# First attention of a four-layer graph kernel: the scaled rows, the logits and the routing choice of older groups are put ahead of the mixing in the orders of ACT, PE and DVE

## The reference

```
h = rmsnorm(layernorm(x), ln1_w)
q, k, v = h @ wq.T, h @ wk.T, h @ wv.T      # 4 heads of 32, 2 kv heads
q, k = rotated(q), rotated(k)
att = softmax(causal(q @ k.T / sqrt(32)))
x2 = layernorm(x) + (att @ v) @ wo.T
flat = rmsnorm(x2, ln2_w)
probs = softmax(flat @ router_w.T)          # 8 experts
tp, ti = top_k(probs, 2)                    # the routing choice
```

## Time and profile before

| | |
|---|---|
| median of 3 runs | 1738.74 us (1738.03 to 1741.6) |
| profiled execution | 1740.67 us |
| its span | 1738.7 us |
| busy in the span | PE 1287.0, DVE 1017.5, POOL 812.2, ACT 740.3 us |
| mean granted TensorE clock | 0.882 of full speed |
| the first attention | from about 380 to 747 us of the span |

### The profile page before, as it was taken

How to read it: one execution, slowest core, us unless ns; L and a number is a source line. 1 busy time by engine, 2 the same in 40 slices (tenths; PEclk the granted TensorE clock), 3 DMA queues, 4 the chain that set the end, 5 groups by cost and what they waited for, 6 DMA issues and landing times. The chain is left out here.

```text
span 1738.7 us, 34925 instructions
## 1 busy us (share of the span) xinstructions
PE 1287.0 (74%) x8909; PEld 1090.6 (63%) x8909; DVE 1017.5 (59%) x3818; ACT 740.3 (43%) x1710; POOL 812.2 (47%) x839
## 2 busy tenths in 40 slices
PE   3988888837677777349999995767773299999930
PEld 2777666726566667238888884545552189888920
DVE  1788888757767776335555553888885122222236
ACT  2555555515655555214444441443432155555510
POOL 3255555561455554614444443277676144445420
PEclk9999999968989988669999997888876599999975
DMA  6100000000000000145656563122211366766647
GB/s 157 23 1 0 0 0 0 1 1 1 20 28 28 25 25 27 40 133 190 201 189 199 191 201 105 55 71 73 71 36 41 104 214 219 218 217 220 218 133 203
DMA packets 134763, 168.57 MB, mean 97 GB/s; under 512 B 17584, under 2 KB 105520, under 8 KB 134704
## 3 DMA queue, kind: packets, MB, share of 16 engines
q1 hardware_dynamic: 98224, 122.49, 23.6%
q0 software_dynamic: 17408, 35.95, 5.9%
q10 hardware_dynamic: 19072, 9.46, 1.9%
HBM read 123.47 MB, written 44.37 MB: 97 GB/s over the span
## 5 line engine op out<-in xcount | busy, mean ns | idle before, releaser
L1602 POOL DMA_INDIRECT rows<-m_yb,m_dsti x288 | 276.6, 960 | 361.1 <-DVE m_dsti L1734 312.5
L1627 PE MATMUL psum<-m_xT,m_w 128*128 128x256 f32 (+1 forms) x864 | 200.2, 381 | 1.3 <-ACT m_xT L1668 1.3
L964 POOL DMA_INDIRECT dispatch<-a_flat,a1r_pos x128 | 129.9, 1015 | 111.4 <-DVE a1r_pos L945 69.4
L964 POOL DMA_INDIRECT dispatch<-g_flat,g1r_pos x128 | 133.2, 1041 | 74.3 <-DVE g1r_pos L945 37.3
L1627 PEld LDWEIGHTS psum<-m_xT,m_w 128*128 128x128 f32 (+1 forms) x864 | 149.1, 179 | 28.9 <-ACT m_xT L1668 1.9
L1701 DVE TENSOR_TENSOR m_yb<-psum,m_w 128x256 f32<-128x256 f32 x72 | 30.6, 425 | 218.6 <-PE psum L1642 218.6
L1683 ACT ACTIVATE m_sg<-psum,m_w 128x256 f32<-128x256 f32 x288 | 117.9, 471 | 92.4 <-PE psum L1632 91.3
L1632 PE MATMUL psum<-m_xT,m_w 128*128 128x256 f32 x576 | 141.2, 389 | 7.4 <-ACT m_xT L1666 7.4
L1642 PE MATMUL psum<-m_w,m_sg 128*128 128x128 f32 x1152 | 140.5, 275 | 0.6 <-DVE m_yb L1701 0.6
L1676 ACT ACTIVATE m_sg<-psum 128x256 f32<-128x256 f32 (+1 forms) x216 | 78.8, 382 | 142.9 <-PE psum L1627 98.5
L1717 DVE TENSOR_TENSOR m_hT<-psum,m_sg 128x256 f32<-128x256 f32 (+1 forms) x216 | 88.4, 422 | 83.7 <-ACT m_sg L1676 81.1
(11 more groups left out here) (250 smaller groups left out, 2971.2 us busy)
## 6 DMA issues: line engine op xcount, KB each, us to landing
m_w<-in_c_wall SPq DMA_DIRECT2D x72, 578.0 KB, 3.6
m_w<-in_c_wall SPq DMA_DIRECT2D x72, 533.0 KB, 3.4
m_xg<-dispatch SPq DMA_DIRECT2D x144, 130.0 KB, 3.5
g1c_y<-rows SPq DMA_DIRECT2D x32, 256.0 KB
fin_y<-rows ACTq DMA_DIRECT2D x32, 256.0 KB, 3.5
rows<-m_yb,m_dsti POOLq DMA_INDIRECT x288, 3.1
out<-x SPq DMA_DIRECT2D x16, 256.0 KB, 3.0
dispatch<-nobody SPq DMA_DIRECT2D x24, 130.0 KB, 6.8
```

The source lines that it names most:

```text
L964: pool.indirect_dma_start(out=dest, out_offset=bass.IndirectOffsetOnAxis(ap=self.pos[:, k, p:p + 1], axis=0), in_=flat[:, p, :], in_offset ...
L1602: pool.indirect_dma_start(out=rows_out, out_offset=bass.IndirectOffsetOnAxis(ap=dsti[j][:, t:t + 1], axis=0), in_=yb[j][:, t, :], in_offse ...
L1627: i = pe.matmul(bank[0:cn, TILE * m:TILE * m + TILE], w[j][:, HID * m + c0:HID * m + c0 + cn], xT[j % 2][:, :], start=(m == 0), stop=True, ...
```

## The change

Three of the four `step` functions of the first attention get another order. No instruction is added, removed or altered.

```diff
--- before.py
+++ after.py
@@ -1197,17 +1197,17 @@
                 def step(g, b):
                     scores(g)
                     head_T(g + 1)
+                    out_T(g - 1)
                     if runs(g - 3):
                         R.tensor_rank(pe, g - 3, bR)
-                    out_T(g - 1)
                     project(g + 1)
                     out_product(g - 1)
+                    flat_T(g - 2, b)
                     probs_T(g, 0)
                     probs_T(g, 1)
-                    flat_T(g - 2, b)
+                    logits(g - 2)
                     turned_T(g + 1)
                     mix(g, b)
-                    logits(g - 2)
                 skewed(pe, step, first=4)
 
             @block.scalar
@@ -1307,14 +1307,14 @@
 
                 def step(g, b):
                     head_T(g + 1)
+                    out_flat(g - 2, b)
+                    out_T(g - 1)
                     exp(g, 0)
                     exp(g, 1)
-                    out_T(g - 1)
-                    head_v(g + 1, 1 - b)
-                    out_flat(g - 2, b)
+                    flat_T(g - 2)
                     probs_T(g, 0)
                     probs_T(g, 1)
-                    flat_T(g - 2)
+                    head_v(g + 1, 1 - b)
                     turned_T(g + 1)
                     head_h(g + 2)
                     out_squares(g - 1)
@@ -1429,11 +1429,11 @@
                     rotated(g + 1, 0)
                     rotated(g + 1, 1)
                     out_x2(g - 1)
+                    if runs(g - 2):
+                        R.vector_choose(dve, g - 2, bR, True)
                     head_stats(g + 3)
                     norm(g)
                     out_ms(g - 1)
-                    if runs(g - 2):
-                        R.vector_choose(dve, g - 2, bR, True)
                 skewed(dve, step, first=4, ahead=3)
                 R.vector_weights(dve, True)
```

## The result

| | before | changed |
|---|---|---|
| median of 4 runs | 1740.17 us (1738.03 to 1743.23) | 1692.07 us (1689.4 to 1699.41) |
| profiled execution, its span | 1740.67, 1738.7 | 1699.41, 1697.5 |
| mean granted clock | 0.882 | 0.879 |

The ratio is 0.9726, 95% interval 0.9696 to 0.9756: 48 us saved, against the 49 of the forecast (1690). The profiled execution of the changed kernel is the slowest of its four; its mean granted clock is 0.879, that of the three others 0.889 to 0.895. Its span is 41.2 us shorter than the one before. It divides so: the first a_mx of the attention is at 403.22 before and 403.43 now, the experts' first DVE instruction at 747.37 and 705.70, and what follows takes 991.3 and 991.8. The whole difference of the two profiled executions lies in the attention, 344.2 us before, 302.3 now.

The account below looks back on a forecast made before the run. A 20.0 us chain across DVE, ACT and PE was taken to pace each turn; without 5.1 us of it DVE would. Savings of 41.7 + 1 + 5.1 + 0.7, say 49 us, gave 1690 us, range 1683 to 1712.

Parts of the forecast that it names:

- The chain and what leaves it: First attention's turn: a 20.0 us chain through DVE, ACT and PE; choice, a_flat and its transpose, together 5.1 us, leave it.
- DVE's 16.33 us as the new bound: Steady turns: DVE's own work paces them, taken as 16.5 us instead of 20.3, saving 41.7 us over 11 turns.
- the rank costs its own few tenths and DVE reads it only after its soft part. Nothing.: PE's rank matmuls, moved behind out_T: no longer held until the choice's end, they add no time to the turn.
- The mixing's margin: PE's mixing done at about +13.6 us of a step, DVE wants it at +14.0: 0.4 us to spare, called pessimistic.
- The logits' margin: PE's logits ready at +8.0 us, DVE wants them at +8.6: 0.6 us to spare, the forecast's thinnest margin.
- POOL: Root and scatters covered by 0.9 us per turn; in the tail, blocks 12.4 us apart, saving 5.1 and 0.7 us.
- The choice beside the scatters: DVE's choice, now beside POOL's scatters, costs nothing; the rival that it holds them up had 5 in 100, 9 us less saved.
- Sum: Whole kernel: 41.7 + 1 + 5.1 + 0.7 = 48.5, say 49 us saved, giving 1690 us by the median.
- The slower rival: PE's clock falls, PE becomes the bound, 3 us above the old turn, about 1770 us; 4 in 100.
- The signs: Trace marks of a right forecast: turn near 16.5 us, DVE busy over 95 in 100, PE's clock 0.95 or more.

Follow-up runs that it names:

- e1: Kernel before with only DVE's order changed (choice moved ahead of the next statistics and norm): 1779.89 us, ratio 1.0202 to the kernel before.
- e2: Changed kernel with DVE's old order put back, so only ACT's and PE's orders new: 1724.83 us, ratio 0.9889 to the kernel before.
- e3: Changed kernel with ACT's old order put back, DVE's and PE's new: 1787.37 us, ratio 1.0260 to the kernel before.
- e8: Changed kernel with PE's rank matmuls directly behind the scores, ahead of head_T and out_T: 1698.59 us, ratio 0.9759 to the kernel before.
- e4: Changed kernel with ACT's copy of v back ahead of fT and the probabilities: 1715.98 us, ratio 0.9849 to the kernel before.

## Why the prediction was right, by its own steps

- **The chain and what leaves it.** Right. The reciprocal's 3.8 us are gone, and e1 to e3 show that the orders belong together: DVE's alone and the other two without ACT's are slower than before, and ACT's and PE's without DVE's bring less than half. PE's order wasn't left out by itself.
- **DVE's 16.33 us as the new bound.** Right for every second turn: 16.46. The forecast's 16.5 for all is the term that was mis-sized: the 11 turns average 16.9, so 37.3 us were saved in them in the profiled execution, not 41.7. The missing 4.4 lie in the turns behind the lower clock (1.7 of them in the turn of step 4), and the step that failed is "the rank costs its own few tenths and DVE reads it only after its soft part. Nothing.": out_T and the rank came late behind slow scores, and DVE waited 0.7 to 1.0 us for them in six of the 11 turns, 5.1 us in all. e8 took this wait away without a shorter median, so it is where the time went in the profile, not a proven gain.
- **The mixing's margin.** The prediction called its 1.81 and 2.61 us the pessimistic case. They weren't: wholly at the lower clock the same groups take 1.94 and 3.52 (e2). The reciprocal was on time all the same, since the transposes ahead of the mixing ran at the upper clock (1.09). The logits' margin of 0.6 us was 0.4, and e4 shows what lies behind it.
- **POOL.** Covered in the loop. The tail was mis-sized: I let landing decide every interval, 12.4 us; the first two are 14.1 and 13.5, since POOL waits 2.80 and 1.54 us for positions whose steps DVE hadn't reached. From step 14 on 3.1 us were saved (76.5 us to the experts' first instruction before, 73.4 now), not 5.8; before step 3 it was 1.5 (44.5 and 43.0), for 1.
- **The choice beside the scatters.** Nothing, as the row at 543.08 shows. The Trainium skill (SBUF — State Buffer, "SBUF: two separate sides") would have had the two engines exclude each other; for these instructions of 0.19 us no scatter inside a choice is longer than 0.97. Beside DVE's addition of the a_t tiles (four of about 0.36 us) one of 1.66 is there in every second turn as before, so the rule may hold for larger ones; no run tested it.
- **Sum.** 37.3 + 1.5 + 3.1 = 41.9 us in the profiled execution, and the whole span gained 41.2; the median gained 48. The agreement of 48 with 49 is thus partly luck: the sum promised these 49 us in the attention's turns and tail, where the trace shows 42. The other executions are 7 to 10 us faster at a granted clock of 0.889 to 0.895 instead of 0.879. None of them was traced, so that their gain lies in turns without a fall of the clock is not shown.
- **The slower rival.** The lower clock came, but for some 7 us in every second turn, 0.89 over the stretch, and its price was 1 us in that turn, not 3 in each.
- **The signs.** Of those listed, the reciprocal, the copy a1r_lg, a_flat and the turn came, the last in half of the turns. Three didn't: the clock was 0.89, not 0.95; the tail's blocks weren't 12.4 us apart; and DVE was busy 88 in 100, not 95. The last was set wrong: with the short gaps between its instructions DVE is busy 14.98 of the 16.46 us even in the turn shown, in which it waits for no one.

## To carry to other kernels

Where a turn is paced by a chain across engines, look in it for pieces that the next link doesn't read, and ask of each engine's queue what its oldest input allows; then move a whole producer chain (scaled rows, transposes, logits, choice) forward together, since a consumer moved alone waits for its producer in the middle of the queue and costs more than it gave. When the chain is gone, the busiest engine's own work is the new bound only where the others keep a margin: reckon every PE term that follows a wait at the clock's lower level too, with a duration from a stretch wholly at that level. One added instruction tells whether an engine paces a loop, but read it turn by turn in the trace, not from the total, and compare the granted clocks of the two traces first.

## What I had not expected of the hardware

Two profiles of one kernel alternate between turns of 16.4 and 17.4 us, because PE's clock falls to its lower level for some 7 us in every second turn, although PE's longest wait over 440 to 620 is 1.6 us and it works 34.3 of 40 us. An instruction of 0.6 us added to the engine that is 88% busy moved the median by 1.4 us (ratios 0.9758 and 0.9764, intervals overlapping). And one set of runs had the kernel before 64 us slower, with waits of 5 us in the traces beside it that the profile ascribes to nothing in the kernel.
